# Expert layer: down products with the features on the partitions

## The chip, the cores and the metric

One core of one Trainium2 chip runs the whole kernel. The metric is the time of one execution in device microseconds; lower is better.

## What is computed

Eight batches of 1024 tokens with 256 features pass through an attention layer and then a mixture of experts; both are followed by a layer norm and a residual sum. The attention layer doesn't change here. Of the reference this matters (xf is the attention layer's output after its own layer norm; 8192 tokens, 256 features, 16 experts with 128 hidden units, the best 8 of 16 weighted per token, and one shared expert):

```python
logits = _l2norm(xf) @ _l2norm(gate_w).T
scores = jax.nn.sigmoid(logits)
topk_scores, topk_idx = jax.lax.top_k(scores, K)
...
g = jnp.einsum('nd,edh->neh', xf, w_gate)
u = jnp.einsum('nd,edh->neh', xf, w_up)
y = jnp.einsum('neh,ehd->ned', jax.nn.silu(g) * u, w_down)
routed = jnp.einsum('ned,ne->nd', y, combine)
shared = jax.nn.silu(xf @ sw_gate) * (xf @ sw_up) @ sw_down
...
x = x + _layernorm(_L0_ffn_ref(_layernorm(x, axis=-1), ...), axis=-1)
```

## The kernel before

Attention fills the first 1540 us, the experts the rest. The expert stage takes the tokens in 16 groups of 512 (`GROUP`), and for each group all 17 experts (`ALL_E`, the shared one last). Every product is made in three parts: each operand is split into a high part and the rest (`_hi`, `_lo`), and high x high, low x high and high x low are summed (`PARTS`).

One expert e of group g goes through these steps:

- TensorE, `gu` (L794): gate and up products, six matmuls each, 128x512 out: the hidden units lie on the partitions, the 512 tokens along the row. Two banks each for g and u.
- ScalarE, `silu` (L1046), into `gate_act`.
- VectorE, `gate`: times u (L1352, u read from PSUM), times the token's weight for this expert, `cb` (L1355). L1357 is the first step for the shared expert.
- ScalarE, `h_hi` (L1057), and VectorE, `h_lo` (L1363): the split of h.
- TensorE, `down` (L808): for each of 4 chunks of 128 tokens three matmuls with h as the weights and w_down (256 columns) moving: 12 matmuls, 128 tokens x 256 features each. They add up over all 17 experts in `y_bank`, two PSUM banks.

TensorE's order is written out: gu(e+2), then down(e). So an expert has two periods between its gate and up products and its down product. At e=7 `lg` (L771) makes the router's logits of the next group with 16 small matmuls. In group 0 four jobs of the attention's output projection (L692) stand between experts.

When a group's sums are complete, ScalarE's `store_y` (L1063, placed at e=1 of the next group) copies `y_bank` into `y`. VectorE makes the layer norm's mean and variance from y (`y_stats`, L1369 and L1372) at e=4 and 5 and 1/sqrt (`y_rstd`, 12 steps, L1246 to L1256) at e=6 and 8. GpSimd's `finish` normalizes y (L1692) and adds the residual (L1696) into `fx_res`. SP's queue loads that residual (`load_res`, L488, at its step 1) and stores the result (`store_out`, L492, at its step 12). The last group is finished by VectorE straight from `y_bank` (L1584 to L1598), for which it waits for the residual, `f_res_loaded`.

SP issues all of this stage's DMAs in order. `load_cb(g, e)` (L481) at its step e waits until the h of expert e-4 is done, so SP's steps run four experts ahead of VectorE. `swap(g+1)` (L469, at step 7) exchanges the 32x32 blocks of the next group's x with 16 DMAs, and VectorE's `turn_x` (L1288, at e=7) transposes within blocks: together they give the transpose of x. `store_comb` (L455) and `f_load_x` (L448) belong to the router and to x of the group after next.

VectorE's other side work in a group: 1/sqrt steps of x's layer norm at e=0, `turn_x` at 7, `xt_lo` and norm steps at 8 and 9, logits at 10 (L1299, L1306), routing steps at 11 to 13, `ln_stats` at 14 and 15, 1/sqrt steps at 16. In each of VectorE's steps this side work stands between `gate` and `h_lo`.

The sequence at the start of the kernel that the prediction reads has the projection jobs (L671, six matmuls of 128x512 each) and V jobs (L680, twelve of 128x256 each).

Of the kernel before, what the change touches and what calls it, by code (L numbers as in the profile page):

```python
# [5 lines left out]
BATCHES, SEQ, D = 8, 1024, 256  # L6
HEADS = 16
DH = D // HEADS
CH = 128
# [89 lines left out]
def both_stages(nc, x, x1, wq, wk, wv, wo, biases, ob, ident_dram, out, comb_dram, gate_w, w_gate, w_up, w_down,  # L99
# [8 lines left out]
    with ctx:  # L108
# [58 lines left out]
        recip = sb("recip", [128, HALF])  # L167
        recip_tmp = sb("recip_tmp", [128, HALF])
        two = sb("two", [128, 1])
        cT = [[sb(f"cT_hi{f}", [128, KD, HALF], F32R), sb(f"cT_lo{f}", [128, KD, HALF], F32R)] for f in range(2)]  # L170
        attn_out = [sb(f"attn_out{f}", [128, HC, D]) for f in range(2)]
        x_res = sb("x_res", [128, HC, D])
# [115 lines left out]
        def over(place, used, name, shape, dt=F32):  # L288
# [40 lines left out]
        f_var, f_rstd, f_newton = sb("f_var", [128, GC]), sb("f_rstd", [128, GC]), sb("f_newton", [128, GC])  # L329
        n2, rnorm, newton_n = sb("n2", [128, GC]), sb("rnorm", [128, GC, 1]), sb("newton_n", [128, GC])  # L330

        names = """f_const_loaded w_hi_ready w_split w_split_late gate_ready gate_chain gate_sq_ready gT_ready gT_once gT_read
            f_x_loaded f_x_normed ln_chain f_mean_ready x_swapped xT_ready xT_hi_ready xT_read sq_ready norm_chain
            lg_ready lg_turned lg_read tanh_ready route_chain comb_turned comb_stored
            gu_ready silu_done gated_done h_done h_hi_done h_ready down_done y_stored y_chain y_mean_ready
            y_normed f_res_loaded out_ready out_stored""".split()
        E = {n: sem(n) for n in names}
        last_normed = sem("last_normed")
# [24 lines left out]
        def _(sp):  # L363
# [109 lines left out]
            def load_cb(g, e):  # L473
# [5 lines left out]
                if not (isinstance(n, int) and n < 4):  # L479
                    wait_apart(sp, E["h_done"], n - 3, f_passed["sp"])  # L480
                sp.dma_start(cb[e % 4][:, :],  # L481
                             comb_row(g, e).partition_broadcast(128)).then_inc(cb_loaded[e % 4], 16)

            def load_res(g):
                wait_apart(sp, E["out_stored"], 16 * (g + 1), f_passed["sp"])
                if g == 0:
                    sp.wait_ge(ctx_split, 4 * BATCHES)
                sp.dma_start(fx_res[:, :, :], x1v[:, bass.ds(g * GC, GC), :]).then_inc(E["f_res_loaded"], 16)  # L488
# [64 lines left out]
            def group(g, first, last):  # L553
                for e in range(EXPERTS):
                    if not (first and e < 4):
                        load_cb(g, e)
                    if g == 1 and e == 5:
                        store_x1(LAST, 0)
                        load_residual(LAST, 1)
                    if g == 1 and e == 11:  # L560
                        store_x1(LAST, 1)
                    if e == 1 and not first:
                        load_res(g - 1)
                    if e == SWAP_AT and not last:
                        swap(g + 1)
                    if e == 13 and g + 2 < GROUPS:
                        wait_apart(sp, E["xT_read"], KD * (g + 2), f_passed["sp"])
                        wait_apart(sp, E["lg_ready"], g + 2, f_passed["sp"])
                        f_load_x(g + 2)
                    if e == 12 and not first:  # L570
                        store_out(g - 1)
                if not last:
                    store_comb(g + 1)

            for g in range(GROUPS):
                group(g, g == 0, g == GROUPS - 1)
            load_res(GROUPS - 1)
            for half in range(2):
                at = slice(half * GC // 2, (half + 1) * GC // 2)
# [7 lines left out]
        def _(pe):  # L587
# [210 lines left out]
            def down(g, par, e):  # L798

                n = ALL_E * g + e  # L800
                pe.wait_ge(E["h_ready"], n + 1)
                if e == 0 and not (isinstance(g, int) and g == 0):
                    pe.wait_ge(E["y_stored"], 2 * g)
                i = (e + par) % 2
                for c in range(GC):
                    for t, (a, b) in enumerate(PARTS):

                        last = mm(y_bank[:, c, :], h[i][a][:, c * CH:(c + 1) * CH], w_exp[b][:, e, 2 * D:3 * D],  # L808
                                  start=(e == 0 and t == 0 and c % 2 == 0), stop=(e == ALL_E - 1 and t == 2),
                                  skip_group_check=True)  # L810
                last.then_inc(E["down_done"], 1)
# [121 lines left out]
        def _(act):  # L933
# [124 lines left out]

            def store_y(g):
                act.wait_ge(E["down_done"], ALL_E * (g + 1))  # L1060
                act.wait_ge(E["out_ready"], g + 1)
                for i in range(2):
                    a_(y[:, 2 * i:2 * i + 2, :], y_bank[:, 2 * i:2 * i + 2, :], ACT.Copy).then_inc(E["y_stored"], 1)  # L1063

# [81 lines left out]
        def _(dve):  # L1146
# [212 lines left out]
            def h_lo(g, par, e):  # L1359
# [3 lines left out]
                v.tensor_tensor(h[i][1][:, :], h32[i][:, :], h[i][0][:, :].bitcast(F32),  # L1363
                                ALU.subtract).then_inc(E["h_ready"], 1)

            def y_stats(g, chunks):
                dve.wait_ge(E["y_stored"], 2 * (g + 1))
                for c in chunks:
                    v.bn_stats(stats_y[:, c, :], y[:, c, :]).then_inc(E["y_chain"], 1)  # L1369
                for c in chunks:  # L1370
                    wait_apart(dve, E["y_chain"], LN * g + c + 1, f_passed["dve"])
                    v.bn_aggr(mv_y[:, c, :], stats_y[:, c, :]).then_inc(E["y_mean_ready"], 1)  # L1372
# [150 lines left out]
            def group(g, par, first, last):  # L1523
                for e in range(ALL_E):
                    gate(g, par, e)
                    if first and 1 <= e <= ALL_E - EARLY:
                        weight_lo(EARLY + e - 1)
                    if first:

                        if e in (3, 9):  # L1530
                            split_lo(LAST, e // 9, 1)
                        if e == 3:
                            sum_recip(LAST, 1, 1)
                        if e in (12, 13):
                            for c in range(2):
                                ln_a_stats(LAST, 0, 2 * (e - 12) + c)
                        if e == 15:
                            for c in range(HC):
                                ln_a_stats(LAST, 1, c)
                        if e in (14, 16):  # L1540
                            for c in range(HC):
                                ln_a_aggr(LAST, (e - 14) // 2, c)
                            seed_a(LAST, (e - 14) // 2)
                    if not last:
                        if e == 0:
                            for n in range(6, 12):
                                ln_rstd(g + 1, n)
                        if e == 7:
                            turn_x(g + 1, 0)
                            turn_x(g + 1, 1)  # L1550
                        if e in (8, 9):
                            xt_lo(g + 1, 1 - par, e - 8)
                        if e in (8, 9):
                            for n in range(6):
                                norm_step(g + 1, 6 * (e - 8) + n)
                        if e == 10:
                            turn_logits(g + 1)
                            scale_logits(g + 1)
                        if e in (11, 12, 13):
                            for n in range(5 * (e - 11), min(5 * (e - 10), ROUTE)):  # L1560
                                route_step(g + 1, n)
                        if e == 13:
                            turn_comb(g + 1)
                    if g + 2 < GROUPS:
                        if e in (14, 15):
                            ln_stats(g + 2, False, (2 * (e - 14), 2 * (e - 14) + 1))
                        if e == 16:
                            for n in range(6):
                                ln_rstd(g + 2, n)
                    if not first:  # L1570
                        if e in (4, 5):
                            y_stats(g - 1, (2 * (e - 4), 2 * (e - 4) + 1))
                        if e in (6, 8):
                            for n in range(6):
                                y_rstd(g - 1, 3 * (e - 6) + n)
                    h_lo(g, par, e)

            for g in range(GROUPS):
# [1 line left out]

            g = GROUPS - 1
            dve.wait_ge(E["down_done"], ALL_E * GROUPS)
            for c in range(GC):
                v.bn_stats(stats_y[:, c, :], y_bank[:, c, :]).then_inc(E["y_chain"], 1)  # L1584
            for c in range(GC):
# [16 lines left out]
        def _(pool):  # L1602
# [85 lines left out]
            def finish(g):  # L1688

                wait_apart(pool, E["y_chain"], LN * (g + 1), f_passed["pool"])  # L1690
                for c in range(GC):
                    gp.tensor_scalar(y[:, c, :], y[:, c, :], mv_y[:, c, 0:1], rstd_y[:, c:c + 1],  # L1692
                                     ALU.subtract, ALU.mult).then_inc(E["y_normed"], 1)
                wait_apart(pool, E["f_res_loaded"], 16 * (g + 1), f_passed["pool"])
                wait_apart(pool, E["y_normed"], GC * (g + 1), f_passed["pool"])
                gp.tensor_tensor(fx_res[:, :, :], y[:, :, :], fx_res[:, :, :], ALU.add).then_inc(E["out_ready"], 1)  # L1696

            pool.sem_inc(x1_ready, 1)
            g.memset(two[:, :], 2.0).then_inc(two_set, 1)
# [117 lines left out]
```

## Time and profile before

| | us |
|---|---|
| median of 3 runs | 2713.37 |
| lowest, highest | 2708.16, 2713.44 |
| profiled execution | 2708.72 |
| its span, first to last instruction | 2706.9 |
| PE busy in the span | 2640.4 (98%) |
| DVE busy | 2247.1 (83%) |
| ACT busy | 1627.1 (60%) |
| POOL busy | 1043.9 (39%) |

All rows come from the profiled execution; times are counted from its first instruction. PE is TensorE, PEld its weight loads, DVE VectorE, ACT ScalarE, POOL GpSimd, SPq the queue of SP. The mean time of one matmul in a row is from its start to its modelled end and overlaps the next one; how far apart matmuls start is read in the chain of waits, where a piece "x6" is the time that six of them take of the chain. The granted clock of TensorE is 1.00 at 2.4 GHz.

### The profile page before, as it was taken

The page shows a single profiled execution, that of the slowest core. Times are in us where ns is not written, and L with a number is a line of the kernel's source. Part 1 is how long each engine was busy: PE and PEld are TensorE (multiplying, and loading weights), DVE is VectorE, ACT ScalarE, POOL GpSimd, SP SyncE. Part 2 cuts the span into 40 slices and gives each one's busy share as a digit, 9 for nine tenths or more (in the row PEclk, how much of TensorE's full clock was granted, in tenths as well). Part 3 has the DMA queues.
Part 4 walks back from the last instruction along what each step waited for, and adds up shares of the span by engine and source line. Part 5 has one row for each costly group of instructions (what it writes and reads, how often), then busy time and mean ns, then how long its engine had stood idle before and what let it go on. Part 6 is the DMA issues. An engine that isn't in the chain of part 4 may idle for free.

```text
span 2706.9 us, 48968 instructions
## 1 busy us (share of the span) xinstructions
PE 2640.4 (98%) x17442; PEld 1728.2 (64%) x17442; DVE 2247.1 (83%) x4635; ACT 1627.1 (60%) x3145; POOL 1043.9 (39%) x1034
## 2 busy tenths in 40 slices
PE   7999999999999999999998999999999999999998
PEld 4344444454454444544543388888888888888887
DVE  7899999999999999999999687766666666666665
ACT  2788888888888888888878833333333333333332
POOL 3142655546535546545457653222222112222211
PEclk7899999999999999999999999999999999999999
DMA  6012233133133232330333324233322333323322
GB/s 145 9 38 63 64 83 76 45 68 68 40 68 68 70 70 59 80 68 29 68 76 95 104 76 118 87 80 92 94 79 83 95 94 91 91 82 92 92 81 59
DMA packets 200844, 205.72 MB, mean 76 GB/s; under 512 B 86808, under 2 KB 149288, under 8 KB 198552
## 3 DMA queue, kind: packets, MB, share of 16 engines
q1 hardware_dynamic: 200024, 202.26, 28.6%
q8 instruction: 138, 2.26, 0.4%
q14 instruction: 106, 0.87, 0.1%
q10 hardware_dynamic: 576, 0.33, 0.1%
HBM read 108.74 MB, written 17.30 MB: 47 GB/s over the span
## 4 chain that ended last, share of the span: by engine, by line
PE 81%; DVE 14%; ACT 3%; issue 2%; DMA 0%; DVEq 0%; SPq 0%; ACTq 0%
PE y_bank L808 14%; PE o_bank L647 14%; PE g_bank L794 14%; PE u_bank L794 14%; DVE score_max L1194 11%; PE st_bank L618 10%; PE sm_bank L637 8%; PE job_bank L637 2%; ACT probs L1092 2%; PE sm_bank L743 2%; DVE qk_parts L1217 1%; PE job_bank L743 1%; DVE row_max L1201 1%; ACT o_sb L995 0%; PE job_bank L771 0%
## 5 line engine op out<-in xcount | busy, mean ns | idle before, releaser
L1092 ACT ACTIVATE probs<-st_bank 128x512 f32<-128x512 f32 x2023 | 1079.2, 605 | 264.9 <-PE st_bank L618 255.2
L1194 DVE TENSOR_REDUCE score_max<-sm_bank 128x1 f32<-128x512 f32 x1601 | 1025.8, 682 | 51.3 <-PE sm_bank L637 40.2
L618 PE MATMUL st_bank<-qk_stack 64*128 64x512 f32 x2023 | 734.9, 424 | 7.5 <-ACT probs L1092 6.7
L637 PE MATMUL sm_bank<-qk_stack 64*128 64x512 f32 x1601 | 649.7, 457 | 21.8 <-DVE score_max L1194 16.4
L647 PE MATMUL o_bank<-probs,v_quad 128*32 128x512 f32 x4096 | 548.0, 607 | 2.8 <-ACT probs L1092 2.1
L618 PEld LDWEIGHTS st_bank<-qk_stack 64*128 64x128 f32 x2023 | 349.6, 185 | 284.1 <-ACT probs L1092 240.7
L637 PEld LDWEIGHTS sm_bank<-qk_stack 64*128 64x128 f32 x1601 | 286.6, 188 | 277.2 <-DVE score_max L1194 248.0
L1046 ACT ACTIVATE gate_act<-g_bank 128x512 f32<-128x512 f32 x272 | 162.4, 597 | 393.3 <-PE u_bank L794 393.3
L1352 DVE TENSOR_TENSOR h<-gate_act,u_bank 128x512 f32<-128x512 f32 x256 | 175.9, 687 | 240.8 <-ACT gate_act L1046 240.6
L1057 ACT ACTIVATE h_hi<-h 128x512 fp32r<-128x512 f32 x272 | 172.0, 632 | 333.8 <-DVE h L1355 316.3
L1194 DVE TENSOR_REDUCE score_max<-job_bank 128x1 f32<-128x512 f32 x447 | 305.0, 682 | 14.2 <-PE job_bank L637 12.9
L808 PE MATMUL y_bank<-f_w_hi,h_hi 128*128 128x256 f32 x1088 | 308.2, 283 | 0.1
L808 PE MATMUL y_bank<-f_w_lo,h_hi 128*128 128x256 f32 x1088 | 307.9, 283 | 0.0
L808 PE MATMUL y_bank<-f_w_hi,h_lo 128*128 128x256 f32 x1088 | 307.8, 283 | 0.0
L1692 POOL TENSOR_SCALAR y<-y,mv_y,rstd_y 128x256 f32<-128x256 f32 x60 | 93.4, 1566 | 459.3 <-DVE rstd_y L1256 459.3
L1685 POOL TENSOR_SCALAR f_x_in<-f_x_in,f_mv,f_rstd 128x256 f32<-128x256 f32 x64 | 94.2, 1482 | 376.7 <-DVE f_rstd L1256 376.7
L1642 POOL TENSOR_TENSOR recip_tmp<-sum_part,recip 128x512 f32<-128x512 f32 x96 | 124.3, 1294 | 294.4 <-DVE recip L1226 289.3
L1363 DVE TENSOR_TENSOR h_lo<-h,h_hi 128x512 fp32r<-128x512 f32 x272 | 186.2, 685 | 46.8 <-ACT h_hi L1057 46.5
L808 PEld LDWEIGHTS y_bank<-f_w_hi,h_hi 128*128 128x128 f32 x1088 | 207.6, 191 | 13.0 <-issue 3.0
L794 PE MATMUL g_bank<-f_xT_hi,f_w_hi 128*128 128x512 f32 x544 | 215.4, 396 | 0.5 <-DVE h L1352 0.5
L794 PE MATMUL g_bank<-f_xT_lo,f_w_hi 128*128 128x512 f32 x544 | 215.0, 395 | 0.0
L808 PEld LDWEIGHTS y_bank<-f_w_hi,h_lo 128*128 128x128 f32 x1088 | 207.7, 191 | 9.8
(280 smaller groups left out, 4866.1 us busy)
## 6 DMA issues: line engine op xcount, KB each, us to landing
cb<-comb_dram SPq DMA_DIRECT2D x256, 256.0 KB, 3.6
qk_stack<-qk_parts SPq DMA_DIRECT2D x180, 256.0 KB, 5.5
o_part<-o_sb SPq DMA_DIRECT2D x64, 128.0 KB, 2.7
sum_part<-o_sb SPq DMA_DIRECT2D x64, 128.0 KB, 2.8
x_res<-in_x SPq DMA_DIRECT2D x16, 512.0 KB, 3.9
x<-x_res SPq DMA_DIRECT2D x16, 512.0 KB, 3.0
f_x_in<-x SPq DMA_DIRECT2D x16, 512.0 KB, 6.2
swapped<-f_x_in SPq DMA_DIRECT2D x256, 32.0 KB, 1.9
```

Source lines behind the costliest of these rows:

```text
L618: mm(bank_of(tile)[:, :], k_stack[q][p][rows, kc * CH:(kc + 1) * CH], q_stack[q][p][rows, f * HALF:(f + 1) * HALF], start=True, stop=True) ...
L637: mm(shared_bank[bank][:, :], q_stack[q][p][rows, tok:tok + CH], k_stack[q][p][rows, half * HALF:(half + 1) * HALF], start=True, stop=True ...
L647: last = mm(o_bank[32 * j:32 * j + 32, :], v_quad[q][:, kc, VW * j:VW * j + 32], probs[0 if kc % 2 == 0 else 1][:, j, :], start=(kc == 0), ...
L794: last = mm(bank[:, :], w_exp[b][:, e, col + k * HID:col + (k + 1) * HID], fxT[par][a][:, k, :], start=(t == 0), stop=(t == len(steps) - 1))
L808: last = mm(y_bank[:, c, :], h[i][a][:, c * CH:(c + 1) * CH], w_exp[b][:, e, 2 * D:3 * D], start=(e == 0 and t == 0 and c % 2 == 0), stop= ...
L1046: a_(gate_act[i][:, :], g_bank[i][:, :], ACT.Silu).then_inc(E["silu_done"], 1)
L1057: a_(h[i][0][:, :], h32[i][:, :], ACT.Copy).then_inc(E["h_hi_done"], 1)
L1092: nc.scalar.activation(probs[kc % 2][:, HEAD_AT[j], :], bank_of(4 * U + j)[:, :], ACT.Exp).then_inc(exp_done, 1)
L1194: v.reduce_max(score_max[f][:, HC * (2 * p + e) + c, half:half + 1], shared_bank[max_bank[n]][:, :], AX_X).then_inc(smax_read, 1)
L1352: v.tensor_tensor(h32[i][:, :], gate_act[i][:, :], u_bank[i][:, :], ALU.mult).then_inc(E["gated_done"], 1)
L1363: v.tensor_tensor(h[i][1][:, :], h32[i][:, :], h[i][0][:, :].bitcast(F32), ALU.subtract).then_inc(E["h_ready"], 1)
L1642: g.tensor_tensor(recip_tmp[:, :], sum_part[f][:, :], recip[:, :], ALU.mult).then_inc(recip_chain, 1)
```

## The change

In groups 0 to 14 the roles in the down product are turned round: w_down's 128 columns are the weights, all 512 tokens of h move, six matmuls of 128x512, and y comes out with the features on the partitions. Before the layer norm y must be turned back: ScalarE copies it as before, VectorE transposes 32x32 blocks (`turn_y`, two operations, e=2 and 3) into `y_turns`, SP exchanges the blocks with 16 DMAs (`swap_y`, its step 11) into `y_tokens`. Both tiles lie over attention's tiles that are no longer in use. `y_stats` moves to e=11 and 12 and waits for the exchange, `y_rstd` to 13 and 14, so that `finish` starts after 14. `store_out` moves from step 12 of the next group to step 3 of the one after that, `load_res` from step 1 to step 6. Group 14 is stored after the loop, and the residual of group 15 is loaded after that store. The last group keeps the old down product and VectorE's own ending.

```diff
@@ SP
+            def swap_y(g):
+                wait_apart(sp, E["y_turned"], KD * (g + 1), f_passed["sp"])
+                wait_apart(sp, E["out_ready"], g + 1, f_passed["sp"])
+                tokens = y_tokens[:, :, :].rearrange("p c (k f) -> p (c k) f", k=KD)
+                for b in range(BLOCKS):
+                    for a in range(BLOCKS):
+                        sp.dma_start(tokens[BLOCK * b:BLOCK * (b + 1), :, BLOCK * a:BLOCK * (a + 1)],
+                                     y_turns[BLOCK * a:BLOCK * (a + 1), :, BLOCK * b:BLOCK * (b + 1)]
+                                     ).then_inc(E["y_swapped"], 16)
...
-                    if e == 1 and not first:
+                    if e == 3 and g > 1:
+                        store_out(g - 2)
+                    if e == 6 and not first:
                         load_res(g - 1)
+                    if e == 11 and not first:
+                        swap_y(g - 1)
...
-                    if e == 12 and not first:
-                        store_out(g - 1)
...
+            store_out(GROUPS - 2)
             load_res(GROUPS - 1)
@@ TensorE, down
+                if g < GROUPS - 1:
+                    for m in range(KD):
+                        for t, (a, b) in enumerate(PARTS):
+                            at = 2 * D + m * 128
+                            last = mm(y_bank[:, 2 * m:2 * m + 2, :].rearrange("p c d -> p (c d)"), w_exp[b][:, e, at:at + 128],
+                                      h[i][a][:, :], start=(e == 0 and t == 0), stop=(e == ALL_E - 1 and t == 2))
+                    last.then_inc(E["down_done"], 1)
+                    return
@@ ScalarE, store_y
-                act.wait_ge(E["out_ready"], g + 1)
+                if g > 0:
+                    act.wait_ge(E["y_turned"], KD * g)
@@ VectorE
+            def turn_y(g, k):
+                dve.wait_ge(E["y_stored"], 2 * g + k + 1)
+                if g == 0:
+                    dve.wait_ge(job_ready["OP"], nth("OP", LAST, 1))
+                else:
+                    dve.wait_ge(E["y_swapped"], 16 * BLOCKS * BLOCKS * g)
+                v.transpose(y_turns[:, :, :].rearrange("p (c k) f -> p k c f", k=KD)[:, k, :, :],
+                            y[:, 2 * k:2 * k + 2, :].rearrange("p i d -> p (i d)").rearrange("p (c f) -> p c f", c=GC)
+                            ).then_inc(E["y_turned"], 1)
...
             def y_stats(g, chunks):
-                dve.wait_ge(E["y_stored"], 2 * (g + 1))
+                if g > 0:
+                    dve.wait_ge(E["y_normed"], GC * g)
+                if g < GROUPS - 1:
+                    dve.wait_ge(E["y_swapped"], 16 * BLOCKS * BLOCKS * (g + 1))
+                else:
+                    dve.wait_ge(E["y_stored"], 2 * (g + 1))
...
-                        if e in (4, 5):
-                            y_stats(g - 1, (2 * (e - 4), 2 * (e - 4) + 1))
-                        if e in (6, 8):
+                        if e in (2, 3):
+                            turn_y(g - 1, e - 2)
+                        if e in (11, 12):
+                            y_stats(g - 1, (2 * (e - 11), 2 * (e - 11) + 1))
+                        if e in (13, 14):
                             for n in range(6):
-                                y_rstd(g - 1, 3 * (e - 6) + n)
+                                y_rstd(g - 1, 6 * (e - 13) + n)
...
             g = GROUPS - 1
             dve.wait_ge(E["down_done"], ALL_E * GROUPS)
+            dve.wait_ge(E["y_normed"], GC * g)
```

In `y_stats` and in GpSimd's `finish` the tile `y` becomes `y_of(g)`, which is `y_tokens` for groups 0 to 14.

## Rows read from the trace of the kernel before

**Rows 1.** Windows: stretch, length, busy PE, PEld, DVE, ACT, POOL; PEclk, DMA share, GB/s.

```profile
1730.00:2090.00 360.00, 360.00 (x2129) 315.89 (x2128) 250.65 (x632) 125.11 (x236) 72.77 (x46) 1.00 0.31 89
```

**Rows 2.** Chain of waits, 2020 to 2034: start us, us, what.

```profile
2021.32 1.43 PE y_bank L808 x12
2022.75 1.39 PE g_bank L794 x6
2024.14 1.36 PE u_bank L794 x6
...
2033.86 0.23 PE y_bank L808 x2
```

**Rows 3.** Chain of waits, 10 to 32 us, attention's first projections.

```profile
16.75 1.62 PE job_bank L671 x6
...
19.73 2.72 PE st_bank L671 x12
...
27.89 1.43 PE job_bank L680 x12
```

**Rows 4.** Chain of waits, the down product after the logits (expert 7).

```profile
2016.94 1.63 PE y_bank L808 x12
```

**Rows 5.** Timeline of DVE, experts 11 to 14: start, us, what [idle before].

```profile
2029.40 0.67 DVE L1363 TENSOR_TENSOR h_lo<-h,h_hi 128x512 fp32r<-128x512 f32 x1
2030.35 0.69 DVE L1352 TENSOR_TENSOR h<-gate_act,u_bank 128x512 f32<-128x512 f32 x1 [0.27 <-ACT gate_act L1046]
...
2034.53 0.69 DVE L1352 TENSOR_TENSOR h<-gate_act,u_bank 128x512 f32<-128x512 f32 x1 [0.49 <-ACT gate_act L1046]
...
2038.71 0.69 DVE L1352 TENSOR_TENSOR h<-gate_act,u_bank 128x512 f32<-128x512 f32 x1 [1.08 <-ACT gate_act L1046]
```

**Rows 6.** Timeline of DVE, experts 4, 6 and 7 of the next group.

```profile
2069.30 0.74 DVE L1369 BATCH_NORM_STATS2 stats_y<-y 128x6 f32<-128x256 f32 x2
2069.96 0.41 DVE L1372 BATCH_NORM_AGGREGATE mv_y<-stats_y 128x2 f32<-128x6 f32 x2
...
2077.66 0.16 DVE L1246 TENSOR_SCALAR var_y<-mv_y 128x4 f32<-128x4 f32 x1
...
2081.84 1.30 DVE L1288 STREAM_TRANSPOSE f_x_in<-swapped 128x512 f32<-128x512 f32 x2
```

**Rows 7.** Timeline of SP's queue in one group: start of issuing, us, what, count.

```profile
2010.18 4.50 SPq L481 DMA_DIRECT2D cb<-comb_dram  x2
...
2065.80 10.40 SPq L469 DMA_DIRECT2D swapped<-f_x_in  x16
```

**Rows 8.** Timeline of POOL, last group.

```profile
2662.03 5.39 POOL L1692 TENSOR_SCALAR y<-y,mv_y,rstd_y 128x256 f32<-128x256 f32 x4 [61.29 <-DVE rstd_y L1256]
2667.61 2.40 POOL L1696 TENSOR_TENSOR f_x_res<-y,f_x_res 128x1024 f32<-128x1024 f32 x1 [0.18 <-POOL y L1692]
```

**Rows 9.** Timeline of DVE, last group: experts 10, 14, 16 and the ending.

```profile
2668.44 2.13 DVE L1355 TENSOR_TENSOR h<-h,cb 128x512 f32<-128x512 f32 x1
...
2684.43 0.69 DVE L1352 TENSOR_TENSOR h<-gate_act,u_bank 128x512 f32<-128x512 f32 x1 [1.38 <-ACT gate_act L1046]
...
2694.32 0.69 DVE L1363 TENSOR_TENSOR h_lo<-h,h_hi 128x512 fp32r<-128x512 f32 x1 [0.84 <-ACT h_hi L1057]
...
2700.97 1.90 DVE L1594 TENSOR_SCALAR y<-y_bank,mv_y,rstd_y 128x256 f32<-128x256 f32 x4
```

**Rows 10.** Timeline of SP's queue, last group.

```profile
2670.10 0.39 SPq L492 DMA_DIRECT2D out<-f_x_res  x1
...
2673.82 0.37 SPq L488 DMA_DIRECT2D f_x_res<-x  x1
```

**Rows 11.** DMA issues of the whole span: count, size, median us to landing.

```profile
x_res<-in_x SPq DMA_DIRECT2D x16, 512.0 KB, 3.9
...
swapped<-f_x_in SPq DMA_DIRECT2D x256, 32.0 KB, 1.9
f_x_res<-x SPq DMA_DIRECT2D x16, 512.0 KB, 5.3
```

More of the change, by code:

```diff
@@ L169, in both_stages @@
         two = sb("two", [128, 1])
+        at5 = (region() + 31) // 32 * 32
         cT = [[sb(f"cT_hi{f}", [128, KD, HALF], F32R), sb(f"cT_lo{f}", [128, KD, HALF], F32R)] for f in range(2)]
@@ L330, in both_stages, with y_of @@
         n2, rnorm, newton_n = sb("n2", [128, GC]), sb("rnorm", [128, GC, 1]), sb("newton_n", [128, GC])
+        y_turns = over(at5, 0, "y_turns", [128, GC * KD, CH])
+        y_tokens = over(at5, 4 * K, "y_tokens", [128, GC, D])
+        def y_of(g):
+            return y if g == GROUPS - 1 else y_tokens
         names = """f_const_loaded w_hi_ready w_split w_split_late gate_ready gate_chain gate_sq_ready gT_ready gT_once gT_read
@@ L334, in both_stages @@
             lg_ready lg_turned lg_read tanh_ready route_chain comb_turned comb_stored
-            gu_ready silu_done gated_done h_done h_hi_done h_ready down_done y_stored y_chain y_mean_ready
+            gu_ready silu_done gated_done h_done h_hi_done h_ready down_done y_stored y_turned y_swapped y_chain y_mean_ready
             y_normed f_res_loaded out_ready out_stored""".split()
@@ L1364, in h_lo @@
                                 ALU.subtract).then_inc(E["h_ready"], 1)
-            def y_stats(g, chunks):
-                dve.wait_ge(E["y_stored"], 2 * (g + 1))
+            def turn_y(g, k):
[7 more added lines that the diff above has]
+                            ).then_inc(E["y_turned"], 1)
+            def y_stats(g, chunks):
+                if g > 0:
[4 more added lines that the diff above has]
+                    dve.wait_ge(E["y_stored"], 2 * (g + 1))
                 for c in chunks:
-                    v.bn_stats(stats_y[:, c, :], y[:, c, :]).then_inc(E["y_chain"], 1)
+                    v.bn_stats(stats_y[:, c, :], y_of(g)[:, c, :]).then_inc(E["y_chain"], 1)
                 for c in chunks:
@@ L1691, in finish @@
                 for c in range(GC):
-                    gp.tensor_scalar(y[:, c, :], y[:, c, :], mv_y[:, c, 0:1], rstd_y[:, c:c + 1],
+                    gp.tensor_scalar(y_of(g)[:, c, :], y_of(g)[:, c, :], mv_y[:, c, 0:1], rstd_y[:, c:c + 1],
                                      ALU.subtract, ALU.mult).then_inc(E["y_normed"], 1)
@@ L1695, in finish @@
                 wait_apart(pool, E["y_normed"], GC * (g + 1), f_passed["pool"])
-                gp.tensor_tensor(fx_res[:, :, :], y[:, :, :], fx_res[:, :, :], ALU.add).then_inc(E["out_ready"], 1)
+                gp.tensor_tensor(fx_res[:, :, :], y_of(g)[:, :, :], fx_res[:, :, :], ALU.add).then_inc(E["out_ready"], 1)
             pool.sem_inc(x1_ready, 1)
```

## Prediction

> **What bounds the kernel now.** I read the windows first: over five of the sixteen expert groups TensorE is busy for the whole 360 us at a granted clock of 1.00 (its 2.4 GHz level), VectorE for 251, ScalarE for 125, GpSimd for 73 [rows 1]. The only thing that shortens this stage is less TensorE time per expert. The chain of waits then shows what an expert is: 12 down products 1.43 us, 6 gate products 1.39, 6 up products 1.36, with no other engine between them, so 4.18 us [rows 2]. The reader is to see two things. Twelve matmuls of 256 columns cost more than six of 512, though the columns are the same (3072): 119 ns each against 227. And gate and up are the same six matmuls of the same shape, yet gate, which comes right after the short ones, is 0.03 slower.
>
> The start of the kernel has a sequence that the change will resemble: eight projection jobs of six 128x512 matmuls with full 128-row weights, a wait between one job and the next, then the V jobs with 256 columns. The first job after an idle stretch takes 1.62, the later ones 1.36 each (2.72 for two), and 256 columns again 1.43 for twelve [rows 3]. So 227 ns is the settled price of a 512-column matmul with its weight load, waits between the sixes that are already met cost nothing, and the extra 0.03 belongs to the first six after a break or after short matmuls.
>
> **The change, part by part.**
>
> *Down products (groups 0 to 14, 17 experts each, 255 in all).* Twelve matmuls with h as weights become six with w_down as weights and h moving: the form of the jobs in [rows 3]. I take 1.36 for 1.43: -0.07. Then gate follows 512-column matmuls, not short ones, so it should settle too: 1.36 for 1.39, -0.03. An expert falls from 4.18 to 4.08: 255 x 0.10 = 25.5 us. Bounds: nothing from the gate part gives 255 x 0.07 = 17.9; a transient moved onto down (1.39) with gate unchanged gives 10.2. I take the upper value, because in [rows 3] seven jobs in a row show no trace of a transient. Down products that follow the 16 small logit matmuls (15 times; now 1.63 in place of 1.43 [rows 4]) or the output projection's 256-column jobs (4 times) keep a transient of 0.03: -0.5. Sum 25.0.
>
> TensorE's page in the Trainium skill (TensorE: Matmul & The Clock Gate, Back-to-back issue gap) gives N/2.4 + 2.5 ns for an isolated warm gap, 109 and 216 ns: by it the change would save 12 x 109.2 - 6 x 215.8 = 15 ns per expert, 4 us in all. [rows 2] measure 119 and 227, so what a matmul costs beyond its columns is larger here than in that formula. The same section's sustained 131 ns at N=512 is far below the 227 of this trace.
>
> *turn_y.* Two VectorE transposes of 128x512 per group, at experts 2 and 3, one each. The same operation takes 1.30 for two [rows 6]. At those experts VectorE has no side work and over 1 us idle, and the lead of h_lo over its down product is larger than at 11 (below). Cost nothing. Its wait (y_stored) is met: ScalarE copies y during expert 1, as now; store_y's new wait on y_turned looks a whole group back. Without that cover it would cost 1.3 x 15 = 20 us.
>
> *swap_y.* 16 DMAs on SP's queue at its step 11, with the shapes of swap: 10.40 us of issuing for 16, each landing 1.9 us after issue [rows 7, 11]. SP reaches its step 11 when expert 7's h is done, here at 2010.18 [rows 7]. So swap_y issues from about 2010.7 to 2021.1 and has landed at 2022.5. y_stats now waits for it at expert 11, where VectorE gets to it just before h_lo at 2029.40 [rows 5]: 6 us spare. Queued behind it on SP is cb for expert 12, issued about 2021.2, landed some 4 later, 2025; VectorE multiplies by it at 2031, right after the gate multiply [rows 5], so 6 us spare as well. The x load behind it (step 13) no longer waits for the store and leaves earlier than now. Cost nothing.
>
> *y_stats and y_rstd* move from experts 4 to 8 to experts 11 to 14. Per pair of chunks 0.74 + 0.41 us, and 12 steps that start 0.20 apart, 1.2 for six [rows 6]. At 11, 12 and 13 VectorE already has routing work: its idle time before the gate multiply of 12, 13 and 14 is 0.27, 0.49 and 1.08 [rows 5]. Adding 1.15, 1.15, 1.2 and 1.2 us at 11 to 14, the next gate multiply is late by 0.9, then 0.9 + 1.15 - 0.49 = 1.6, then 1.6 + 1.2 - 1.08 = 1.7. h_lo of expert 11 ends at 2030.07 and its down product starts at 2033.86 [rows 2, 5]: a lead of 3.8. h_lo of expert 13 ends 1.08 before 2038.71, and its down product comes two periods of 4.18 after that of expert 11, at 2042.2: a lead of 4.6. It would be 1.6 + 1.2 = 2.8 late, the worst of the four together with its neighbours, and the shorter period takes 0.2: 1.6 us remain. TensorE doesn't wait. Cost nothing, 1.6 us from costing something.
>
> *finish on GpSimd* starts at expert 14, not 8. Four multiplications 5.39 and one add 2.40 [rows 8]. While that add runs, a VectorE operation with two SBUF inputs waits for its end: 2.13 for 0.69 [rows 9]. In the middle groups this falls on expert 16 or 0 of the next group, with a lead over 4 us: nothing. store_out at SP's step 3 waits for the add, which ends before cb 4 is due. load_res at step 6 has eight experts until it is read.
>
> *The tail.* finish(14) now runs at the very end. Gate multiply of expert 14 starts at 2684.43, its second multiply ends at 2685.84; six rstd steps, 2687.05; GpSimd 5.39 + 0.18 + 2.40: 2695.05. h_lo of expert 16, at 2694.32 [rows 9], is held to about 2695.6: last down product 0.6 late. The store of group 14 goes out at 2695.15, and only when it has landed does load_res(15) leave: now these two issues are 3.72 apart [rows 10], so 2698.9. It lands 3.9 (as the x_res load) to 5.3 (as f_x_res itself, among the loads of cb) after that [rows 11]: 2702.8 to 2704.2. VectorE now starts the last normalization at 2700.97 [rows 9], and would have to wait: +1.8 to +3.2, the 0.6 within it. With SP free of other issues I take the low end, +2.0.
>
> **Sum** against the profiled execution (2708.72, span 2706.9): -25.5 + 0.5 + 2.0 = -23.0, so 2685.7. That execution is 4.65 under the median of the runs shown (2713.37); two of three lie at 2713.4, one at 2708.2. Against the median the sum gives 2690.4, and this is the forecast.
>
> **The rivals.**
>
> A. Forecast, both gains: 2690.4 (2685 if the runs fall low). Chance 0.66.
>
> B. Gate stays at 1.39: the transient is gate's own. For it: gate is slow in every expert of the trace, whatever VectorE and ScalarE do. Against: the up products and seven of the eight jobs in [rows 3]. Saving 17.9 - 2.5 = 15.4: 2698.0 (2693 low). Chance 0.17.
>
> C. The change doesn't do what it says: a 512-column matmul with h moving costs twice the 256-column one (240 ns), because the cost goes by columns here. Nothing saved, tail +2.0: 2715.4. Against it [rows 2, 3], with 1.36 for the same form. The page's formula above comes near this, with 2711 by its 4 us. Chance 0.05.
>
> D. Slower: VectorE's wait for y_swapped. It stands in order before h_lo of expert 11, and cb 12 stands behind swap_y on SP. If an issue took 1.4 us instead of 0.65, swap_y would be out at 2033.1 and cb 12 landed at 2036.8, for a multiply wanted at 2031; with 0.7 for it, 2.8 of side work and 0.6 for h_lo, h_lo of expert 12 would end at 2040.9, and its down product is due at 2038.0: 2.9 late, 15 x 2.9 = 43, -23 + 43 = +20: 2733. It overtakes the gain at 1.5 us per group, which is an issue of 1.3 us. For it: the margins are only 6 us, and no row has two swaps in one group. Against: the blocks have swap's sizes on both sides. Chance 0.06.
>
> The rest, 0.06, is a mixture: a small wait of TensorE at experts 12 to 14, up to 1 us per group (up to 2705), or a longer tail (+5).
>
> **How the numbers follow.** The likeliest is A at 2690. The range 2683 to 2700 holds A at either level of the runs and with a tail from 1.5 to 4, and B, and leaves out C, D and half of the mixture. What a measurement of this kernel can tell from no change is about 0.2%, 5.4 us. Faster 0.88 (A, B, most of the rest), same 0.06 (C and a bit of the rest), slower 0.06 (D).
>
> **What would show it.** In the chain after: down x6 1.36, gate x6 1.36, up x6 1.36, a period of 4.08; groups 70.1 us apart rather than 71.8. DVE transposes of 0.65 to 0.69 at experts 2 and 3 and no wait for y_swapped. In SP's rows 16 issues of 0.65 twice per group. TensorE busy through all groups without a wait for h_lo. At the end: the add on GpSimd within 2 us of the last h_lo, the load of f_x_res after the last store, and VectorE idle before the last normalization. A gate at 1.39 makes it B, a down at 1.43 C, TensorE waiting for h_lo once in a group D. The forecast is too low if less is left of expert 13's lead than my 1.6 us.

## The result and the profile after

The changed kernel takes 2687.65 us (median of 4 runs, 2684.54 to 2690.47), against 2713.37 (2708.16 to 2713.44). The ratio to the kernel before is 0.9915, 95% interval 0.9903 to 0.9927. The forecast was 2690.4. The profiled execution took 2687.88 with a span of 2686.1, 20.8 less than the span before.

The windows of the kernel after come first. The columns are the stretch, its length, busy time of PE, PEld, DVE, ACT and POOL, the granted clock, DMA share and GB/s.

```profile
1730.00:2090.00 360.00, 360.00 (x1651) 296.11 (x1650) 251.77 (x657) 127.24 (x241) 69.64 (x45) 1.00 0.37 100
```

As in [rows 1], TensorE is busy for all 360 us at a granted clock of 1.00. Its matmuls in the window fall from 2129 to 1651. VectorE does about the same (251.77 us for 250.65), the DMA queues some more (share 0.37 for 0.31). So the stage is still TensorE's own chain, only with a shorter period. The chain of waits of one group shows the pieces (start, us, what; L832 is the new down product, L816 gate and up, L793 the logits):

```profile
2008.33 0.57 PE job_bank L793 x16
2008.90 1.60 PE y_bank L832 x6
2010.51 1.38 PE g_bank L816 x6
2011.89 1.36 PE u_bank L816 x6
2013.25 1.36 PE y_bank L832 x6
2014.61 1.36 PE g_bank L816 x6
2015.97 1.36 PE u_bank L816 x6
...
2078.53 0.57 PE job_bank L793 x16
```

Where [rows 2] had 1.43, 1.39 and 1.36, all three are now 1.36: 4.08 us per expert. From one logits piece to the next it is 70.20 us. Only the down product right after the logits is longer: 1.60, where [rows 4] had 1.63, and the gate after it takes 1.38.

VectorE at experts 11 to 15 is where the prediction saw the margin shrink (start, us, operation, idle before it in brackets):

```profile
2021.74 0.66 DVE L1395 TENSOR_TENSOR h_lo<-h,h_hi 128x512 fp32r<-128x512 f32 x1
2022.32 0.68 DVE L1384 TENSOR_TENSOR h<-gate_act,u_bank 128x512 f32<-128x512 f32 x1
...
2026.88 0.68 DVE L1384 TENSOR_TENSOR h<-gate_act,u_bank 128x512 f32<-128x512 f32 x1
...
2030.55 0.68 DVE L1395 TENSOR_TENSOR h_lo<-h,h_hi 128x512 fp32r<-128x512 f32 x1
2031.15 0.68 DVE L1384 TENSOR_TENSOR h<-gate_act,u_bank 128x512 f32<-128x512 f32 x1
...
2038.40 0.69 DVE L1389 TENSOR_TENSOR h<-gate_act,u_bank 128x512 f32<-128x512 f32 x1 [0.33 <-ACT gate_act L1077]
```

The idle times of [rows 5] are gone, the gate multiplies of experts 12, 13 and 14 follow at once, and VectorE is back on time at expert 16. h_lo of expert 13 ends at 2031.23, and its down product starts in the chain at 2033.65. TensorE never waited for it.

SP's queue shows both exchanges (L499 is swap_y in this group, L477 the swap of x that comes after it):

```profile
2002.85 11.21 SPq L499 DMA_DIRECT2D y_tokens<-y_turns  x16
2014.49 0.81 SPq L489 DMA_DIRECT2D cb<-comb_dram  x2
...
2056.73 10.78 SPq L477 DMA_DIRECT2D swapped<-f_x_in  x16
```

The swap of x takes 10.78 for its 16, where [rows 7] have 10.40. The last block of y is issued from 2013.44 and lands at 2015.43, 2.0 later. VectorE begins the statistics at 2020.74, so 5.3 us after that.

The ending is the part that got longer. This is the chain of waits of the last 22 us:

```profile
2665.09 0.11 POOL y_tokens L1742
...
2666.56 3.93 POOL y_tokens L1742 x3
...
2670.64 2.46 POOLq L108
...
2673.17 2.95 DMA out<-f_x_res
...
2676.20 3.89 DMA f_x_res<-x
...
2680.18 1.90 DVE y L1644 x4
```

The kernel now ends on group 14's `finish`, its store, and the load of group 15's residual, in a row. Before, it ended on the last down product and VectorE's statistics. Beside it, on GpSimd and VectorE:

```profile
2670.67 2.41 POOL L1746 TENSOR_TENSOR f_x_res<-y_tokens,f_x_res 128x1024 f32<-128x1024 f32 x1 [0.18 <-POOL y_tokens L1742]
```

```profile
2672.29 1.34 DVE L1395 TENSOR_TENSOR h_lo<-h,h_hi 128x512 fp32r<-128x512 f32 x1 [0.84 <-ACT h_hi L1088]
...
2680.18 1.90 DVE L1644 TENSOR_SCALAR y<-y_bank,mv_y,rstd_y 128x256 f32<-128x256 f32 x4 [0.64 <-DMA f_x_res<-x]
```

h_lo of expert 16 takes 1.34 where [rows 9] have 0.69, since it is held until GpSimd's add ends at 2673.08, and the normalization waits 0.64 for the residual.

Two starts of matmuls and the end divide the span (starts from the timeline of PE, us):

| | first down product | last matmul of the last gate product | end |
|---|---|---|---|
| before | 1550.16 | 2690.38 | 2706.9 |
| after | 1552.54 | 2668.34 | 2686.1 |

The expert stage falls from 1140.22 to 1115.80, so by 24.42. The ending grows from 16.5 to 17.75, by 1.2. The stretch up to the first down product, nearly all of it attention and the same code in both kernels, took 2.4 longer in this one execution; the section on the changed kernel's second profile shows where. 2.4 - 24.4 + 1.2 = -20.8.

### The profile page after: what moved, and what is told of

Its sections match the earlier page's. It is cut to its first block, busy times and chain, and to the rows that moved or that the text cites. A ratio compares the mean times of both kernels' runs of the same rounds, so it can differ in the third digit from the quotient of the medians.

```text
span 2686.1 us, 46266 instructions
## 1 busy us (share of the span) xinstructions
PE 2618.1 (97%) x15912; PEld 1650.1 (61%) x15912; DVE 2237.8 (83%) x4665; ACT 1626.3 (61%) x3145; POOL 1037.2 (39%) x1034
## 4 chain that ended last, share of the span: by engine, by line
PE 80%; DVE 14%; ACT 3%; issue 2%; DMA 0%; POOL 0%; POOLq 0%; DVEq 0%; SPq 0%; ACTq 0%
PE o_bank L669 14%; PE g_bank L816 14%; PE u_bank L816 14%; PE y_bank L832 13%; DVE score_max L1226 11%; PE st_bank L640 10%; PE sm_bank L659 8%; PE job_bank L659 2%; ACT probs L1124 2%; PE sm_bank L765 2%; DVE qk_parts L1249 1%; PE job_bank L765 1%; DVE row_max L1233 1%; PE y_bank L839 1%; ACT o_sb L1026 0%
## 5 line engine op out<-in xcount | busy, mean ns | idle before, releaser
L1742 POOL TENSOR_SCALAR y_tokens<-y_tokens,mv_y,rstd_y 128x256 f32<-128x256 f32 x60 | 83.5, 1402 | 805.3 <-DVE rstd_y L1288 805.3
L816 PE MATMUL g_bank<-f_xT_hi,f_w_hi 128*128 128x512 f32 x544 | 212.3, 390 | 0.5 <-DVE h L1384 0.5
L816 PE MATMUL g_bank<-f_xT_lo,f_w_hi 128*128 128x512 f32 x544 | 212.0, 390 | 0.0
L816 PE MATMUL g_bank<-f_xT_hi,f_w_lo 128*128 128x512 f32 x544 | 211.7, 389 | 0.0
L816 PE MATMUL u_bank<-f_xT_hi,f_w_lo 128*128 128x512 f32 x544 | 211.6, 389 | 0.0
L816 PE MATMUL u_bank<-f_xT_hi,f_w_hi 128*128 128x512 f32 x544 | 211.6, 389 | 0.0
L816 PE MATMUL u_bank<-f_xT_lo,f_w_hi 128*128 128x512 f32 x544 | 211.6, 389 | 0.0
L832 PE MATMUL y_bank<-h_hi,f_w_hi 128*128 128x512 f32 x510 | 200.3, 393 | 0.0
L832 PE MATMUL y_bank<-h_lo,f_w_hi 128*128 128x512 f32 x510 | 198.8, 390 | 0.0
```

Source lines behind the costliest of these rows:

```text
L816: last = mm(bank[:, :], w_exp[b][:, e, col + k * HID:col + (k + 1) * HID], fxT[par][a][:, k, :], start=(t == 0), stop=(t == len(steps) - 1))
L832: last = mm(y_bank[:, 2 * m:2 * m + 2, :].rearrange("p c d -> p (c d)"), w_exp[b][:, e, at:at + 128], h[i][a][:, :], start=(e == 0 and t = ...
```

## The experiments

The theory: six matmuls of 512 columns cost less than twelve of 256, because each matmul with its weight load costs something beyond its columns, and matmuls that follow the short ones run slower for a while. The rest of the change is hidden, except at the ending. The rivals: the gain came from h no longer being the weights, from the side work having moved, or the slower gate was gate's own.

### Down products in halves

```diff
                     for m in range(KD):
-                        for t, (a, b) in enumerate(PARTS):
-                            at = 2 * D + m * 128
-                            last = mm(y_bank[:, 2 * m:2 * m + 2, :]..., w_exp[b][:, e, at:at + 128], h[i][a][:, :], ...)
+                        for half in range(2):
+                            for t, (a, b) in enumerate(PARTS):
+                                last = mm(y_bank[:, 2 * m + half, :], w_exp[b][:, e, at:at + 128],
+                                          h[i][a][:, half * D:(half + 1) * D], ...)
```

> The changed kernel with one size altered: w_down stays the weights and h moves, but in two halves of 256 columns, so 12 matmuls of 128x256 per expert in place of 6 of 128x512. Theory (the number of matmuls with their weight loads is what cost the time, and gate pays a transient after short ones): down 1.43 us, gate 1.39, up 1.36 in the chain, period 4.18, time 24 to 25 us above the changed kernel, about 2712. Rival (it was h as the weights, fresh from ScalarE and VectorE, that was slow): down 1.36, gate 1.36, time stays at 2688.

Measured: 2711.38 us (10 runs), ratio to the kernel before 1.0007 (0.9998 to 1.0017). Its chain of waits:

```profile
2023.22 1.43 PE y_bank L833 x12
2024.65 1.39 PE g_bank L816 x6
2026.04 1.36 PE u_bank L816 x6
2027.40 1.43 PE y_bank L833 x12
```

With w_down as the weights and h moving, but at 256 columns, the whole gain is gone, and the three pieces are those of [rows 2]. The stretch from the first down product to the last gate product is 1140.22 us, to the hundredth that of the kernel before. With equal widths it makes no difference here which operand is the weights; the width does. The slower gate comes back with the short matmuls before it.

### The old down product, everything else new

```diff
-                if g < GROUPS - 1:
+                if False:
                     for m in range(KD):
```

> The changed kernel with the old down product in all groups (12 matmuls of 128x256, h as weights); everything else of the change stays: turn_y, swap_y, the moved statistics, stores and loads. y is then turned although it needs no turning, so the output of groups 0 to 14 is not the reference's. Theory: all of the gain is TensorE's; the rest of the change costs about 1.2 us at the tail and nothing elsewhere, so the time is that of the kernel before plus 1, about 2713, with a period of 4.18. Rival (part of the gain came from moving the side work away from the experts 4 to 10): below the kernel before, 2700 to 2708.

Measured: 2712.44 us (10 runs), ratio 1.0005 (0.9996 to 1.0015). In the chain of waits:

```profile
2024.60 1.43 PE y_bank L839 x12
2026.04 1.39 PE g_bank L816 x6
```

The stage takes 1140.22 again, the ending 17.74. So turn_y, swap_y, 240 more DMAs and the moved statistics neither cost nor gain anything in the stage as long as TensorE's period is the old 4.18. The rival that moving the side work brought part of the gain falls.

### Up products in halves

```diff
-                for bank, col in ((g_bank[i], 0), (u_bank[i], D)):
-                    for t, (k, a, b) in enumerate(steps):
-                        last = mm(bank[:, :], ..., fxT[par][a][:, k, :], ...)
+                for t, (k, a, b) in enumerate(steps):
+                    mm(g_bank[i][:, :], ..., fxT[par][a][:, k, :], ...)
+                for half in range(2):
+                    at = slice(half * D, (half + 1) * D)
+                    for t, (k, a, b) in enumerate(steps):
+                        last = mm(u_bank[i][:, at], ..., fxT[par][a][:, k, at], ...)
```

> The changed kernel with the up products in halves of 256 columns (12 matmuls of 128x256), gate and down untouched. Theory (the transient belongs to whatever 512-column matmuls follow the short ones): up 1.43, down 1.39, gate 1.36, period 4.18, about 25 us above the changed kernel, 2713. Rival 1 (the transient is gate's own and shows when the stream is uneven): up 1.43, down 1.36, gate 1.39, same total. Rival 2 (no transient outside the old kernel): up 1.43, down 1.36, gate 1.36, period 4.15, plus 18 us, 2706.

Measured: 2710.6 us (10 runs), ratio 1.0004 (0.9995 to 1.0014). The chain of waits:

```profile
2019.88 1.39 PE y_bank L836 x6
2021.27 1.36 PE g_bank L815 x6
2022.62 1.43 PE u_bank L820 x12
```

Now up is the 1.43, and the 1.39 has moved to down, which follows it. Gate stays at 1.36. The total can't tell the theory from rival 1, but the rows do: the slower six are those that come after short matmuls, whatever they compute. The expectation's second rival, no transient outside the old kernel, falls with them.

### Down products in quarters

```diff
+                        for c in range(GC):
+                            for t, (a, b) in enumerate(PARTS):
+                                last = mm(y_bank[:, 2 * m + c // 2, (c % 2) * CH:(c % 2 + 1) * CH], w_exp[b][:, e, at:at + 128],
+                                          h[i][a][:, c * CH:(c + 1) * CH], ...)
```

> The changed kernel with the down product in 24 matmuls of 128x128 (128 columns of h each). It tells what a matmul costs beyond its columns. If a fixed 13 ns comes on top of the columns at every size (227 = 213 + 13, 120 = 107 + 13), a matmul takes 67 ns, down 1.60, and the time is 255 x 0.27 = 69 us above the changed kernel, 2757. If a weight load of 128 columns sets a floor near the 107 to 120 of the 256-column matmuls, down takes 2.6 to 2.9 us and the time is 255 x 1.3 = 330 us above, about 3020.

Measured: 3034.7 us (one run), 347 above the changed kernel, where the floor gave 330 and the fixed 13 ns gave 69. The chain of waits:

```profile
2025.55 1.45 PE g_bank L816 x6
2027.00 1.38 PE u_bank L816 x6
2028.38 2.63 PE y_bank L833 x24
```

24 matmuls of 128 columns take 2.63 us, 110 ns each, hardly less than 119 for twice the columns. So it isn't a fixed 13 ns on top of the columns: at 128 columns the stream is bound by something of about 110 ns per matmul. The transient grows with it: gate 1.45, and even up 1.38.

The starts of single matmuls narrow this down. These are the first of the 24, right behind the up product:

```profile
2028.22 0.22 PE L833 MATMUL y_bank<-h_hi,f_w_hi 128*128 128x128 f32 x1
2028.27 0.28 PE L833 MATMUL y_bank<-h_lo,f_w_hi 128*128 128x128 f32 x1
2028.39 0.27 PE L833 MATMUL y_bank<-h_hi,f_w_lo 128*128 128x128 f32 x1
```

The first gives way after 57 ns, those behind it after 109 to 115. In the kernel before it is 113 ns for the first of the 12, then 119 or 120. 57, 113 and 227 ns go with the columns, 0.44 ns each. So not every matmul brings an extra cost: it appears when short ones stand in a row, up to 7 ns each at 256 columns and about 54 at 128. What makes it isn't shown.

The Trainium skill (TensorE: Matmul & The Clock Gate, LDWEIGHTS) gives a weight load as columns/1.2 ns, which makes an estimate of 107 ns for 128 columns; the 110 measured here is near it. That the floor is the weight load is inferred from this, and so is any link from it to the transient. The runs vary the moving columns and keep one 128-column load per matmul; none changes the load.

### The exchange of y two experts later

```diff
-                    if e == 11 and not first:
-                        swap_y(g - 1)
...
+                    if e == 13 and not first:
+                        swap_y(g - 1)
```

> The changed kernel with swap_y at SP's step 13 in place of 11, two experts (8.2 us) later; VectorE still wants y at expert 11. In the changed kernel the last block lands 4.7 us before VectorE is there, so it would now be 3.6 us late. Theory (TensorE has 2.5 us of lead over h_lo at its least, at experts 12 and 13): VectorE waits 3.6 us for y_swapped, TensorE about 1.1 us per group, 15 x 1.1 = 17 us above the changed kernel, 2705. Rival (the lead is not used up that way, the wait is hidden): 2688. Rival (each microsecond of VectorE's wait goes to TensorE): 15 x 3.6 = 54, 2742.

Measured: 2702.18 us (5 runs), ratio to the kernel before 0.9965 (0.9951 to 0.9979). The stage takes 1130.09, 14.3 more than in the changed kernel: groups 1 to 14 grow by 0.6 to 1.8 each, 1.02 in the mean, and the last group not at all. Its queue and VectorE at expert 11, in a group that grows by 1.15:

```profile
2013.40 10.76 SPq L499 DMA_DIRECT2D y_tokens<-y_turns  x16
```

```profile
2021.32 1.15 DVE L1351 MAX8 top<-scores 128x8 f32<-128x16 f32 x4
2025.61 0.75 DVE L1416 BATCH_NORM_STATS2 stats_y<-y_tokens 128x6 f32<-128x256 f32 x2 [3.14 <-DMA y_tokens<-y_turns]
```

and in the chain of waits:

```profile
2031.16 0.67 DVE h_lo L1395
2031.88 1.66 PE y_bank L832 x6
```

VectorE waits 3.14 us here and 3.2 in the mean of the 15 exchanges. In this group 1.15 of it reaches TensorE, over the down products of experts 11 to 14 (behind the wait the product of expert 12 also takes 1.66 for 1.36): the rest is the lead. Both rivals fall. The expectation counted 4.7 us between landing and use; it is 5.3, so the exchange was to be 2.9 us late, and not 3.6. This is the wait of rival D of the prediction: the mechanism exists, and about 2 us of it are free.

### An earlier ending of group 14

```diff
-                        if e in (11, 12):
+                        if e in (11, 12) and not last:
                             y_stats(g - 1, (2 * (e - 11), 2 * (e - 11) + 1))
-                        if e in (13, 14):
+                        if e in (13, 14) and not last:
...
+                        if e == 10 and last:
+                            y_stats(g - 1, range(GC))
+                        if e == 11 and last:
+                            for n in range(12):
+                                y_rstd(g - 1, n)
```

> The changed kernel with, in the last group alone, y_stats for group 14 at expert 10 and y_rstd at expert 11 in place of 11 to 14, so that GpSimd's finish(14), the store and the last residual's load come three experts earlier. Theory (the tail of the change costs 0.65 us for h_lo held by GpSimd's add and 0.64 for the load of the last residual): h_lo of expert 16 takes 0.69 again, no DMA in the chain that ended last, the stretch from the up products of expert 16 to the end 16.3 us in place of 17.5; time 1.2 us below the changed kernel, less than its runs spread, so the rows decide. Rival (the ending is held by something else, such as VectorE's own chain): the stretch stays at 17.5.

Measured: 2686.7 us (4 runs, 2683.77 to 2689.51), ratio to the kernel before 0.9905 (0.989 to 0.992). The time alone can't be told from the changed kernel's. The rows can. The chain of waits at the end:

```profile
2674.92 0.70 DVE h_lo L1395
...
2675.67 1.71 PE y_bank L839 x12
...
2677.41 0.49 DVE stats_y L1639 x2
...
2681.57 1.90 DVE y L1649 x4
```

No DMA and no GpSimd stands in it, and the ending takes 16.51 us, as in the kernel before. The whole 1.2 us was the placement of group 14's `finish`. The add still holds an h_lo, but that of expert 14, which has a lead:

```profile
2662.25 2.40 POOL L1751 TENSOR_TENSOR f_x_res<-y_tokens,f_x_res 128x1024 f32<-128x1024 f32 x1 [0.18 <-POOL y_tokens L1747]
```

```profile
2662.97 2.23 DVE L1395 TENSOR_TENSOR h_lo<-h,h_hi 128x512 fp32r<-128x512 f32 x1 [0.70 <-ACT h_hi L1088]
```

This kernel computes the same as both others and is the best of them by its rows.

### The changed kernel again

> The changed kernel once more, on the same chip as the two others, to compare stretches. Theory: the expert stage from the first down product to the up products of expert 16 of the last group is 1116 us again, as in its first profile, and what differs between executions (some 2 to 5 us) lies in the attention stage before it.

Measured: 2687.96 us (4 runs, 2685.29 to 2690.63), ratio 0.991 (0.9895 to 0.9925). The stage took 1115.80 again, and so it did in the kernel with the earlier ending. What differs is when the stage begins. The first gate product in the chain of waits of the changed kernel's first profile:

```profile
1542.32 1.58 PE g_bank L816 x6
```

and of this one:

```profile
1545.04 1.59 PE g_bank L816 x6
```

Over the nine profiles of this case it begins between 1538.4 and 1545.0. The record shows where that comes from. Near 1418 the same VectorE instruction starts within 1.3 us in all nine; the spread arises between 1480 and 1530, at the end of attention, with the granted clock. The windows of PE there (length, busy PE, granted clock, DMA share, GB/s) in the kernel before, in this profile and in the one with the later exchange:

```profile
1480.00:1530.00 50.00, 43.51 (x283) 0.97 0.28 77
```

```profile
1480.00:1530.00 50.00, 45.07 (x253) 0.83 0.26 71
```

```profile
1480.00:1530.00 50.00, 42.29 (x285) 1.00 0.28 77
```

Where the mean is under 1.00, the clock stood at its 1.2 GHz level for part of that window. Profiles with a mean of 1.00 start the first gate product at 1539.0 and 1539.4, those with 0.97 at 1538.4 and 1539.9, with 0.90 at 1541.8 and 1542.2, with 0.86 at 1543.2, with 0.83 at 1544.9 and 1545.0. The changed kernel's first profile has 0.90 and the kernel before 0.97: this goes with the 2.4 us by which attention was longer. Why the clock stays low longer in some executions isn't shown.

## Why the prediction was right

*Down products, 255 x 0.07, and gate, 255 x 0.03.* Right in mechanism and in size: 1.43 to 1.36, 1.39 to 1.36, and the two come and go together with the short matmuls, as the experiments with the down and the up products in halves show. The sum of the two less transients was 25.0; the stage fell by 24.42. The missing 0.6 lies mostly in the group's expert 7, where I charged a transient of 0.03 once: the rows show the down product after the logits only 0.03 faster than before and the gate behind it only 0.01, so 0.06 of the 0.10 is lost, 15 times, where I had counted 0.03.

*The choice of the upper value,* from the projection jobs of [rows 3], was the step that mattered. Rival B (gate stays at 1.39) was the likely error and would have given 7.6 us less.

*The issue-gap formula of the Trainium skill* (TensorE: Matmul & The Clock Gate, Back-to-back issue gap; 15 ns per expert, 4 us in all) fell short here: the measured saving is 96 ns per expert (24.42 / 255). It adds 2.5 ns per matmul to the columns; this kernel pays 119 ns where it has 109, twelve times, 227 where it has 216, six times, and the slower gate on top.

*turn_y, swap_y, y_stats, y_rstd at no cost.* Right; the run with the old product and everything else new shows a stage of 1140.22, unchanged. The margins were off. I gave swap_y 6 us of spare time (6.9 by my own figures) and it had 5.3, since SP took 0.8 longer to issue it (11.21 for 10.40) and VectorE, no longer held up, came 0.8 earlier. I gave h_lo of expert 13 a rest of 1.6, and it had 2.4, because GpSimd's add no longer holds VectorE at expert 10. The prediction says where the hold moves to and doesn't count that it leaves expert 10, where the timeline of DVE before had

```profile
2023.72 2.44 DVE L1306 TENSOR_TENSOR logits<-lg_turns,rnorm 128x64 f32<-128x64 f32 x1
```

and the changed kernel needs 0.23 for the same operation.

*The tail, +2.0.* Right in mechanism, too large: 1.2 measured. The term that was too large is the step from store to load, which I took as 3.72 from [rows 10]. There SP had 3.12 us of loads of cb to issue in between; now the load left 3.03 after the store. h_lo of expert 16 was held 0.65 for my 0.6, the load took 3.89 for my 3.9.

*The sum.* Stage and tail together gave -23.2 where I had -23.0. That they agree so closely is luck: the stage saved 0.6 less than my 25.0 and the tail cost 0.8 less than my 2.0. Against the profiled execution before (2708.72) the changed one took 2687.88 instead of 2685.7. That is the 2.4 us before the stage, less the 0.2. It is also why a forecast against the median is only as good as the level of the median: more runs of the kernel before, 25 beside the first experiments, have a median of 2710.52, and 8 beside the later ones 2712.02, not 2713.37. The same sum from 2710.52 is 2687.5, and 2687.65 was measured.

*Rivals C and D.* C is refuted by the 1.36. D was a real mechanism with a margin that held (an issue took 0.65 to 0.70, not 1.4); the exchange two experts later shows what it costs once the margin is spent.

## What to carry to other kernels

Where TensorE is the bound and two layouts of a product have the same columns in total, take the one with fewer, wider matmuls: here 119 ns for 256 columns against 227 for 512, and 110 for 128, all with a weight load per matmul. Look at the pieces of the chain by product: a product that is slower than its twin of the same shape can show a cost that what comes before it leaves behind, and here it went when the short matmuls went. When finishing work is moved later in a pipeline, do the last round by hand: it has no next round to hide in, and there it cost 1.2 us that an earlier slot for one group gave back.

## What the runs showed of the hardware

- A matmul of 128 moving columns takes 110 ns in a stream with one 128-column weight load each, one of 256 columns 119, one of 512 columns 227. Not in a row, right behind 512-column matmuls, the same widths take 57 and 113 ns. After 24 of the shortest, the next two products of six 512-column matmuls run slower (gate 1.45, up 1.38 for 1.36); after twelve of 256, the next one (1.39).
- The expert stage repeats to the hundredth of a microsecond over executions and kernels: 1140.22 in three kernels, 1115.80 in three profiles of two kernels. The spans of the changed kernel's two profiles differ by 2.7 us, and their first gate products start 2.7 apart: the spread comes from before the stage, from the end of attention, where the mean granted clock between 1480 and 1530 lies between 0.83 and 1.00 over the nine profiles. A gain of this stage could be read to 0.01 us from one profile, where ten timed runs give 0.1%.
- A GpSimd add with two SBUF operands holds a VectorE operation with two SBUF operands until it ends (1.34 and 2.23 us for 0.69), not one that reads PSUM: the L1389 multiply of expert 16, at 2670.76, kept its 0.69 beside the add that began at 2670.67. The Trainium skill has this as an exclusive lock on a shared port pair (SBUF — State Buffer, Who interferes with whom), and the traces agree for the add. GpSimd's four multiplications of `finish`, which read SBUF too, held no such VectorE operation: h_lo at 2037.41 took its 0.66 while they ran from 2034.78 to 2040.37.
